# Layer-0 result split straight from its PSUM bank instead of from an SBUF copy, in a fused recommendation tower

## Chip, cores and metric

One core of one Trainium2 chip. The metric is the device time of one execution in microseconds (us), lower is better; a kernel is told by the median of several executions.

## What is computed

For 512 samples, 39 embedding rows of 16 numbers are gathered from tables (`x0`, 39 x 16 for each sample). Three cross layers follow; each multiplies the 39 rows with the rows of the layer before, column by column of the 16, and contracts all pairs with a filter:

```python
e = jnp.stack([tbl_0[ids[:, 0]], ..., tbl_38[ids[:, 38]]], axis=1)   # 512 x 39 x 16
x0, xk = e, e
for W in [f0, f1, f2]:            # 39*39 x 128, 128*39 x 128, 128*39 x 128
    z = jnp.einsum('bfd,bgd->bfgd', x0, xk).reshape(b, f * g, d)
    cur = jnp.einsum('bpd,pm->bmd', z, W)
    outs.append(cur); xk = cur
z = jnp.sum(jnp.concatenate(outs, axis=1), axis=-1)                  # 512 x 384
h = relu(concat([z, dense_ctx]) @ W_top1 + b_top1)
y = relu(h @ W_top2 + b_top2) @ W_top3
```

## The kernel before

**Blocks and tiles.** The 512 samples go in 16 blocks of 32 samples (512 columns, sample by d); a block is four tiles of 128 columns. Layer 0 of block b+1 is made while layer 1 of block b runs. The order on every engine is written out by hand: constants such as `HIGH_AT` name a place (t, n), which is tile t and the n-th group that this engine works on in that tile.

**Layer 0.** SyncE writes the gathered rows to DRAM (`rows_to_dram`) and reads them back in the layout that layer 0 needs (`load_rows`: one DMA into `x0t`, three into `pairs`). `load_rows(b)` waits for `l0_done`, because `pairs` is a single buffer and layer 0 of the block before must have read it. VectorE multiplies `x0t` into `pairs` in seven pieces (`z0`, L435); the first two of block b+2 are made as early as (3, 2) and (3, 3) of block b. Four of the pieces are split into a high and a low fp32r half: ScalarE rounds (`z0h`, L574), VectorE or, for piece 2, GpSimd subtracts (`z0l`, L442 and L383). TensorE sums the seven pieces into the bank `ps0` (`layer0`, called at the places of `L0_AT`, piece 0 at (0, 6), 1 at (0, 8), 4 at (1, 7) and last piece 5 at (2, 3)).

**The layer-0 result** is the left operand of layer 1 and is also split. ScalarE copies the whole bank to SBUF (`load_cur0`, `x1f`, L565), rounds it tile by tile to `x1h` (`high_part`, L581), and VectorE subtracts, `x1l = x1f - x1h` (`low_part`, L449). VectorE also sums `x1f` over d into `s0` (`sum_cur0`, L453). Tiles 0 to 2 are split during block b for block b+1, tile 3 in block b+1 itself: its high part at (0, 0), its low part at (1, 3).

**Layer 1.** In each tile TensorE makes ten groups of four filters, three matmuls each (hi x w1h, hi x w1l, lo x w1h: L769, L770, L773), into a bank of `psd` (two banks) or `psa` (three), by the pattern `adaadadaad`. VectorE takes a "d" group with one tensor_tensor (L474, the first of a tile) or four scalar_tensor_tensor (L486), which frees the bank; ScalarE takes an "a" group with four scaled copies (L618), and GpSimd adds four of those six (L379). GpSimd also makes `x0d` (L364) and starts the gathers of block b+3 (L346). After its first group of a tile, VectorE reduces the four partial results of the tile before (`finish_tile`, L459), for which it waits until ScalarE and GpSimd are through with that tile. One more matmul (`grams`, L747) prepares layer 2.

**After the last block** layer 2 and the small network on top run as before; they reuse `x1f` as the tile `s2`.

Of the kernel before, what the change touches and what calls it, by code (L numbers as in the profile page):

```python
# [25 lines left out]
F32 = mybir.dt.float32  # L26
F32R = mybir.dt.float32r
I32 = mybir.dt.int32
ALU = mybir.AluOpType
# [5 lines left out]
BB = 32  # L35
# [49 lines left out]
assert all(sorted(at.values()) == SPLIT for at in (ZH_AT, ZH_AT_FIRST))  # L85


CUR0_AT, SUM_AT = (2, 3), (2, 3)
HIGH_AT = {(2, 4): 0, (3, 0): 1, (3, 2): 2}
SCALARS_AT = {(2, 5): 0, (3, 1): 1, (3, 3): 2}  # L90
LOW_AT = {(2, 3): 0, (3, 1): 1, (3, 2): 2}
# [36 lines left out]
def build(nc, tables, ids, w0a, w0b, w1, w2, wt1, bt1, wt2, bt2, wt3, dense, mask, ident, out):  # L128
# [4 lines left out]
    with ExitStack() as ctx:  # L133
        def sb(name, shape, dt=F32):
            return ctx.enter_context(nc.sbuf_tensor(name, shape, dt))

        def sem(name):
            return ctx.enter_context(nc.semaphore(name))
# [22 lines left out]
        pairs = sb("pairs", [128, L0T, COLS])  # L161
        z0h = sb("z0h", [128, NS * COLS], F32R)
        z0l = sb("z0l", [128, NS * COLS], F32R)
        x1f = sb("x1f", [128, COLS])
        x1h = sb("x1h", [128, COLS], F32R)
        x1l = sb("x1l", [128, COLS], F32R)

# [15 lines left out]
        h2 = parts[:, 0, 0:H2T, :]  # L183
        wt2_sb = parts[:, 1, 0:H1T * H2T * 128 // B, :].rearrange("p a n -> p (a n)").rearrange("p (k n) -> p k n", k=H1T)
        dense_sb = x0t[0:16, :]
        s2 = x1f
        y_sb = s0[0:1, :]


# [37 lines left out]
        z0l_pool = sem("z0l_pool")  # L227
        l0_done = sem("l0_done")
        tr_done = sem("tr_done")
        x1f_ready = sem("x1f_ready")  # L230
        x1h_ready = sem("x1h_ready")
        x1l_ready = sem("x1l_ready")
        x0c_ready = sem("x0c_ready")
# [191 lines left out]
        def _(dve):  # L425
# [19 lines left out]
            def low_part(b, t):  # L445

                dve.wait_ge(x1h_ready, b * TILES + t + 1)
                c = slice(128 * t, 128 * t + 128)
                dve.tensor_tensor(x1l[:, c], x1f[:, c], x1h[:, c].bitcast(F32), ALU.subtract).then_inc(x1l_ready, 1)  # L449

            def sum_cur0(b, at):
                dve.wait_ge(x1f_ready, b + 1)
                dve.tensor_reduce(s0[:, at], x1f[:, :].rearrange("p (b d) -> p b d", d=D), AX.X, ALU.add)  # L453

            def finish_tile(T, t):

# [6 lines left out]
            def block_of(b, ahead, ahead2, at=None):  # L463
                for t in range(TILES):
                    T = b * TILES + t
                    groups = [g for g in range(NG) if PATTERN[t][g] == "d"]
                    for n, g in enumerate(groups):
# [23 lines left out]
                        if n == 0:  # L491
# [3 lines left out]
                            if t or not starts(b):  # L495
# [1 line left out]
                                dve.wait_ge(pool_adds, bp * NADD + ADD_OFF[tp + 1])  # L497
                                dve.wait_ge(acc_steps, 2 * (bp * ND + D_OFF[tp + 1]))
                                finish_tile(T - 1, tp)
                        if t == 1 and n == 3:  # L500
                            low_part(b, TILES - 1)
                        z0_at = Z0_AT_FIRST if starts(b) else Z0_AT
                        if ahead:
# [24 lines left out]
                dve.tensor_tensor(w1l[:, c], w1raw[:, c], w1h[:, c].bitcast(F32), ALU.subtract).then_inc(w1l_ready, 1)  # L528
            for k in range(L0T):
                z0(0, k)  # L530
            for t in range(3):
                low_part(0, t)
            sum_cur0(0, slice(0, BB))
            block_of(0, True, True, slice(BB, 2 * BB))
            with dve.Fori(1, NBLK - 2) as b:
                block_of(b, True, True, bass.ds((b + 1) * BB, BB))
# [21 lines left out]

        @block.scalar
        def _(act):  # L560
            def load_cur0(b):
                act.wait_ge(l0_done, b + 1)
                if not starts(b):
                    act.wait_ge(x1l_ready, b * TILES)
                act.activation(x1f[:, :], ps0[:, :], ACT.Copy).then_inc(x1f_ready, 1)  # L565
                act.wait_ge(x1f_ready, b + 1)

            def pair_high_part(b, k):

                i = SPLIT.index(k)  # L570
# [5 lines left out]
            def high_part(b, t):  # L576

                c = slice(128 * t, 128 * t + 128)
                if not starts(b):
                    act.wait_ge(y_d, (b - 1) * ND + D_OFF[t + 1])  # L580
                act.activation(x1h[:, c], x1f[:, c], ACT.Copy).then_inc(x1h_ready, 1)  # L581

            def scalars(b, t):
                act.wait_ge(tr_done, b + 1)
# [10 lines left out]
            def block_of(b, ahead):  # L595
                for t in range(TILES):
                    T = b * TILES + t
                    groups = [g for g in range(NG) if PATTERN[t][g] == "a"]
                    for n, g in enumerate(groups):
# [30 lines left out]
                        if t == 0 and n == 2:  # L630
                            scalars(b, 3)
                        if ahead:
                            if (t, n) == CUR0_AT:
                                load_cur0(b + 1)
                            if (t, n) in HIGH_AT:
                                high_part(b + 1, HIGH_AT[t, n])
                            if (t, n) in SCALARS_AT:
                                scalars(b + 1, SCALARS_AT[t, n])
# [11 lines left out]
            for k in range(3):  # L650
                c = slice(k * third, (k + 1) * third)
                act.activation(w1h[:, c], w1raw[:, c], ACT.Copy).then_inc(w1h_ready, 1)
            load_cur0(0)
            for t in range(3):
                high_part(0, t)
            act.wait_ge(w1l_ready, 3)
# [48 lines left out]
        def _(pe):  # L705
            def layer0(b, k):

                if k == 0 and not starts(b):
                    pe.wait_ge(x1f_ready, b)
                pe.wait_ge(z0_ready, b * L0T + k + 1)  # L710
                if k in SPLIT and not starts(b):

                    i = SPLIT.index(k)
                    pe.wait_ge(z0h_ready, (b - 1) * NS + i + 1)
                    if k == ON_POOL:
                        pe.wait_ge(z0l_pool, b)
                    else:
                        pe.wait_ge(z0l_ready, (b - 1) * (NS - 1) + i)
                    c = slice(COLS * i, COLS * i + COLS)
                    w = slice(M * i, M * i + M)  # L720
                    pe.matmul(ps0[:, :], w0h[0:ROWS, w], z0h[0:ROWS, c], start=False, stop=False)  # L721
                    pe.matmul(ps0[:, :], w0h[0:ROWS, w], z0l[0:ROWS, c], start=False, stop=False)
                    op = pe.matmul(ps0[:, :], w0l[0:ROWS, w], z0h[0:ROWS, c], start=False, stop=(k == L0_END))
                    if k == L0_END:
                        op.then_inc(l0_done, 1)
                    return
                rows = F * len(range(SPT * k, min(SPT * k + SPT, SHIFTS)))
                op = pe.matmul(ps0[:, :], w0s[0:rows, k, :], pairs[0:rows, k, :], start=(k == 0), stop=(k == L0_END))  # L728
                if k == L0_END:
                    op.then_inc(l0_done, 1)  # L730
# [70 lines left out]


            pe.wait_ge(mlp_in, 16 * 3)
            pe.wait_ge(x1f_ready, NBLK)
            pe.wait_ge(x0c_ready, NBLK * TILES)
            banks = [ps0, pst, psa[0], psa[1]][:H1T]
            for m, y in enumerate(banks):
# [98 lines left out]
```

## Time and profile before

| | |
|---|---|
| three runs | 773.94, 777.85, 781.08 us; median 777.85 |
| span of the profiled execution | 775.4 us, so 2.45 us under the median |
| VectorE busy | 687.4 us, 89% |
| TensorE matmul busy | 658.1 us, 85% |
| ScalarE busy | 536.4 us, 69% |
| GpSimd busy | 509.0 us, 66% |
| one block in the middle of the run | about 42 us |

The profiled execution has one number, its span; no time of its own beside that is given, so sums are made against the span and carried over to the median. Busy is an average over the whole run. Inside the blocks VectorE is busy for 41.5 of 42 us, and the other engines wait for one another in a fixed pattern that repeats from block to block. A duration shown for an instruction includes time in which it has started and stands still for a resource.

### The profile page before, as it was taken

What the parts mean: (1) busy time and instruction counts of PE and PEld (TensorE: products, weight loads), DVE (VectorE), ACT (ScalarE), POOL (GpSimd) and SP (SyncE); (2) the same over time, 40 slices, a digit from 0 to 9 for tenths busy, and PEclk for the clock granted to TensorE, in tenths of its full rate; (3) what the DMA queues carried; (4) which work ended last, traced back from release to release, by engine and by line L of the source; (5) the groups of instructions that cost most, each with busy time, mean ns of one, the idle gap of its engine ahead of it and who ended that gap; (6) DMA issues with size and microseconds to landing.
All of it is one profiled execution on the core that took longest, in us unless ns stands there. A gap on an engine that the chain in (4) does not pass through costs nothing.

```text
span 775.4 us, 12234 instructions
## 1 busy us (share of the span) xinstructions
PE 658.1 (85%) x2571; PEld 471.9 (61%) x2571; DVE 687.4 (89%) x1110; ACT 536.4 (69%) x1862; POOL 509.0 (66%) x462
## 2 busy tenths in 40 slices
PE   0768888898989888898989898878989898998988
PEld 0246656566766666666766675656666666666563
DVE  1448899999999999999999999979999998999880
ACT  2055768496876767686859686665859696788672
POOL 6755868586767767685868676766868644455340
PEclk9899999999999999999999999998999999999999
DMA  7540404040412214040404031220404041300200
GB/s 190 109 103 6 102 2 100 7 97 8 86 18 54 51 23 82 2 103 1 98 7 96 9 82 23 46 53 7 98 7 96 9 106 31 97 2 1 64 1 0
DMA packets 57049, 40.27 MB, mean 52 GB/s; under 512 B 35455, under 2 KB 39885, under 8 KB 57032
## 3 DMA queue, kind: packets, MB, share of 16 engines
q1 hardware_dynamic: 51206, 38.73, 22.4%
q0 software_dynamic: 5120, 1.29, 1.9%
q10 hardware_dynamic: 706, 0.06, 0.1%
q8 instruction: 6, 0.10, 0.0%
q14 instruction: 11, 0.09, 0.0%
HBM read 38.13 MB, written 1.94 MB: 52 GB/s over the span
## 4 chain that ended last, share of the span: by engine, by line
PE 40%; DMA 18%; issue 17%; DVE 16%; POOL 4%; SPq 2%; ACT 2%; DVEq 1%; ACTq 0%; POOLq 0%
DMA pairs<-x_rows 17%; DVE parts L486 7%; PE psd L769 5%; PE psa L769 4%; PE psa L773 4%; PE psa L770 4%; PE psd L773 4%; PE psd L770 3%; DVE z0l L442 3%; PE ps L728 2%; DVE pairs L435 2%; PE psg L747 2%; PE ps L721 2%; POOL parts L379 1%; ACT prods L618 1%
## 5 line engine op out<-in xcount | busy, mean ns | idle before, releaser
L618 ACT ACTIVATE prods<-psa,x0c 128x128 f32<-128x128 f32 x1024 | 296.8, 393 | 60.5 <-PE psa L773 52.8
L459 DVE TENSOR_REDUCE cur<-parts 128x128 f32<-128x2048 f32 x64 | 245.8, 3840 | 4.1 <-POOL parts L379 3.9
L486 DVE SCALAR_TENSOR_TENSOR parts<-psd,x0c,parts 128x128 f32<-128x128 f32 x704 | 194.3, 342 | 6.4 <-PE psd L773 6.4
L379 POOL TENSOR_TENSOR parts<-parts,prods 128x512 f32<-128x512 f32 x128 | 167.9, 1311 | 40.5 <-ACT prods L618 39.0
L769 PE MATMUL psa<-w1h,x1h 128*128 128x512 f32 x384 | 173.8, 453 | 9.9 <-ACT prods L618 8.8
L346 POOL DMA_INDIRECT emb<-tables,idx x140 | 146.5, 1047 | 32.1 <-issue 19.3
L769 PE MATMUL psd<-w1h,x1h 128*128 128x512 f32 (+1 forms) x256 | 112.6, 440 | 50.0 <-DVE parts L486 48.0
L773 PE MATMUL psa<-w1h,x1l 128*128 128x512 f32 x384 | 152.6, 397 | 0.0
L770 PE MATMUL psa<-w1l,x1h 128*128 128x512 f32 x384 | 152.4, 397 | 0.0
L379 POOL TENSOR_TENSOR parts<-prods 128x512 f32<-128x512 f32 x64 | 84.1, 1313 | 99.2 <-ACT prods L618 89.8
L618 ACT ACTIVATE parts<-psa,x0c 128x128 f32<-128x128 f32 x512 | 143.3, 422 | 2.3 <-ACT x1f L565 2.2
L574 ACT ACTIVATE z0h<-pairs 117x512 fp32r<-117x512 f32 x60 | 38.0, 633 | 117.9 <-DVE pairs L435 116.6
L769 PEld LDWEIGHTS psd<-w1h,x1h 128*128 128x128 f32 x256 | 48.5, 189 | 95.6 <-DVE parts L486 82.5
L435 DVE TENSOR_TENSOR pairs<-x0t,pairs 117x512 f32<-117x512 f32 (+1 forms) x112 | 87.9, 789 | 18.9 <-DMA pairs<-x_rows 18.4
L773 PE MATMUL psd<-w1h,x1l 128*128 128x512 f32 (+1 forms) x256 | 98.4, 384 | 0.0
L770 PE MATMUL psd<-w1l,x1h 128*128 128x512 f32 (+1 forms) x256 | 98.3, 384 | 0.0
L769 PEld LDWEIGHTS psa<-w1h,x1h 128*128 128x128 f32 x384 | 72.6, 189 | 39.9 <-ACT prods L618 16.0
L770 PEld LDWEIGHTS psa<-w1l,x1h 128*128 128x128 f32 x384 | 72.8, 189 | 22.1 <-issue 4.6
L773 PEld LDWEIGHTS psa<-w1h,x1l 128*128 128x128 f32 x384 | 72.5, 189 | 17.9
L449 DVE TENSOR_TENSOR x1l<-x1f,x1h 128x128 fp32r<-128x128 f32 x64 | 56.6, 886 | 4.6 <-ACT x1h L581 4.6
L728 PE MATMUL ps<-pairs,w0s 117*128 117x512 f32 (+1 forms) x104 | 55.8, 627 | 3.8 <-DVE pairs L435 3.7
L474 DVE TENSOR_TENSOR parts<-psd,x0c 128x512 f32<-128x512 f32 x64 | 43.8, 684 | 14.5 <-issue 14.4
(87 smaller groups left out, 753.3 us busy)
## 6 DMA issues: line engine op xcount, KB each, us to landing
pairs<-x_rows SPq DMA_DIRECT2D x30, 546.0 KB
pairs<-x_rows SPq DMA_DIRECT2D x15, 468.0 KB
x0t<-x_rows SPq DMA_DIRECT2D x16, 234.0 KB
emb<-tables,idx POOLq DMA_INDIRECT x140
pairs<-x_rows SPq DMA_DIRECT2D x8, 156.0 KB
x_rows<-emb SPq DMA_DIRECT2D x14, 72.0 KB
wt_sb<-w_top SPq DMA_DIRECT2D x1, 768.0 KB, 12.1
prods<-w SPq DMA_DIRECT2D x1, 704.0 KB, 4.8
```

Source lines behind the costliest of these rows:

```text
L346: pool.indirect_dma_start(emb[0:n, c, :], None, tables, bass.IndirectOffsetOnAxis(idx[0:n, c:c + 1], 0)).then_inc(gathered, 16)
L379: pool.tensor_tensor(parts[:, t % 2, 1, :], first, prods[:, p % P_RING, :], ALU.add).then_inc(pool_adds, 1)
L435: dve.tensor_tensor(pairs[0:rows, k, :], x0t[0:rows, :], pairs[0:rows, k, :], ALU.mult).then_inc(z0_ready, 1)
L449: dve.tensor_tensor(x1l[:, c], x1f[:, c], x1h[:, c].bitcast(F32), ALU.subtract).then_inc(x1l_ready, 1)
L459: dve.tensor_reduce(cur1[:, t % 2, :], parts[:, t % 2, :, :].rearrange("p k (j m) -> p m (k j)", m=M), AX.X, ALU.add).then_inc(c1_ready, 1)
L474: dve.tensor_tensor(parts[:, t % 2, 0, :].rearrange("p (j m) -> p j m", m=M), y[:, :].rearrange("p (j m) -> p j m", m=M), x0c[:, t, GF * g ...
L486: op = dve.scalar_tensor_tensor(acc, y[:, M * j:M * j + M], x0c[:, t, GF * g + j:GF * g + j + 1], acc, ALU.mult, ALU.add)
L618: op = act.activation(dst[:, M * j:M * j + M], y[:, M * j:M * j + M], ACT.Copy, scale=x0c[:, t, GF * g + j:GF * g + j + 1])
L728: op = pe.matmul(ps0[:, :], w0s[0:rows, k, :], pairs[0:rows, k, :], start=(k == 0), stop=(k == L0_END))
L769: pe.matmul(y[:, 0:n], hi, w1h[:, c], start=True, stop=False)
L770: pe.matmul(y[:, 0:n], hi, w1l[:, c], start=False, stop=False)
L773: pe.matmul(y[:, 0:n], lo, w1h[:, c], start=False, stop=True).then_inc(full, 1)
```

## The change

The bank `ps0` is no longer copied to `x1f`; the sum over d, the four high parts and the four low parts read `ps0` itself. ScalarE and VectorE are never to read the bank at the same time, so they take turns by semaphores: the first high part waits for the sum (`s0_summed`), the high part of tile t waits for the low part of tile t-1 (`x1l_ready`), and a low part waits for its high part as before. Layer 0 of the next block overwrites the bank, so its first piece now waits for all four low parts of the block before, where it waited for the copy. The low part of tile 3 is moved from (1, 3) to (0, 0), behind `finish_tile`. In the first block the sum is moved ahead of the low parts. `s2` gets another tile.

```diff
-CUR0_AT, SUM_AT = (2, 3), (2, 3)
+SUM_AT = (2, 3)
 ...
-        s2 = x1f
+        s2 = parts[:, 0, 2, :]
 ...
-                dve.tensor_tensor(x1l[:, c], x1f[:, c], x1h[:, c].bitcast(F32), ALU.subtract).then_inc(x1l_ready, 1)
+                dve.tensor_tensor(x1l[:, c], ps0[:, c], x1h[:, c].bitcast(F32), ALU.subtract).then_inc(x1l_ready, 1)
             def sum_cur0(b, at):
-                dve.wait_ge(x1f_ready, b + 1)
-                dve.tensor_reduce(s0[:, at], x1f[:, :].rearrange("p (b d) -> p b d", d=D), AX.X, ALU.add)
+                dve.wait_ge(l0_done, b + 1)
+                dve.tensor_reduce(s0[:, at], ps0[:, :].rearrange("p (b d) -> p b d", d=D), AX.X,
+                                  ALU.add).then_inc(s0_summed, 1)
 ...
-                        if t == 1 and n == 3:
+                        if t == 0 and n == 0:
                             low_part(b, TILES - 1)
 ...
+            sum_cur0(0, slice(0, BB))
             for t in range(3):
                 low_part(0, t)
-            sum_cur0(0, slice(0, BB))
 ...
-            def load_cur0(b):
-                act.wait_ge(l0_done, b + 1)
-                if not starts(b):
-                    act.wait_ge(x1l_ready, b * TILES)
-                act.activation(x1f[:, :], ps0[:, :], ACT.Copy).then_inc(x1f_ready, 1)
-                act.wait_ge(x1f_ready, b + 1)
 ...
+                if t == 0:
+                    act.wait_ge(s0_summed, b + 1)
+                else:
+                    act.wait_ge(x1l_ready, b * TILES + t)
                 if not starts(b):
                     act.wait_ge(y_d, (b - 1) * ND + D_OFF[t + 1])
-                act.activation(x1h[:, c], x1f[:, c], ACT.Copy).then_inc(x1h_ready, 1)
+                act.activation(x1h[:, c], ps0[:, c], ACT.Copy).then_inc(x1h_ready, 1)
 ...
-                            if (t, n) == CUR0_AT:
-                                load_cur0(b + 1)
 ...
-            load_cur0(0)
 ...
                 if k == 0 and not starts(b):
-                    pe.wait_ge(x1f_ready, b)
+                    pe.wait_ge(x1l_ready, b * TILES)
 ...
-            pe.wait_ge(x1f_ready, NBLK)
+            pe.wait_ge(x1l_ready, NBLK * TILES)
```

## Rows read from the trace of the kernel before

**Rows 1.** The page, costliest groups: line, engine, tiles, count | busy us, mean ns | idle before.

```profile
L449 DVE TENSOR_TENSOR x1l<-x1f,x1h 128x128 fp32r<-128x128 f32 x64 | 56.6, 886 | 4.6 <-ACT x1h L581 4.6
```

**Rows 2.** Single lines of the kernel: count, duration ns min/median/max, first and last start.

```profile
L449 DVE TENSOR_TENSOR x1l<-x1f,x1h x64: 273/972/1511, 40.8 to 700.8; 128x128 fp32r<-128x128 f32 x64
...
L486 DVE SCALAR_TENSOR_TENSOR parts<-psd,x0c,parts x704: 329/341/365, 47.4 to 717.3; 128x128 f32<-128x128 f32 x176
...
L474 DVE TENSOR_TENSOR parts<-psd,x0c x64: 675/680/693, 42.6 to 710.3; 128x512 f32<-128x512 f32 x64
```

**Rows 3.** Chain of waits, 290 to 380 us: start us, us, what.

```profile
288.32 13.49 DMA pairs<-x_rows
...
323.77 0.50 PE psa L769
```

**Rows 4.** Timeline of SyncE's queue: start us, us, instruction; "xN" merges several.

```profile
328.45 0.74 SPq L292 DMA_DIRECT2D x0t<-x_rows  x1
```

**Rows 5.** Timeline of VectorE, one block from `z0` to `z0`.

```profile
301.84 0.69 DVE L435 TENSOR_TENSOR pairs<-x0t,pairs 117x512 f32<-117x512 f32 x1
...
304.43 3.82 DVE L459 TENSOR_REDUCE cur<-parts 128x128 f32<-128x2048 f32 x1
...
312.20 1.18 DVE L435 TENSOR_TENSOR pairs<-x0t,pairs 117x512 f32<-117x512 f32 x1
...
318.27 2.11 DVE L442 TENSOR_TENSOR z0l<-pairs,z0h 117x512 fp32r<-117x512 f32 x1
...
334.25 1.02 DVE L449 TENSOR_TENSOR x1l<-x1f,x1h 128x128 fp32r<-128x128 f32 x1
...
342.13 1.51 DVE L449 TENSOR_TENSOR x1l<-x1f,x1h 128x128 fp32r<-128x128 f32 x1
343.56 0.68 DVE L435 TENSOR_TENSOR pairs<-x0t,pairs 117x512 f32<-117x512 f32 x1
```

**Rows 6.** Timeline of GpSimd beside those VectorE rows.

```profile
301.74 0.92 POOL L346 DMA_INDIRECT emb<-tables,idx  x1 [0.16 <-issue]
...
311.54 1.30 POOL L379 TENSOR_TENSOR parts<-parts,prods 128x512 f32<-128x512 f32 x1
...
317.87 0.74 POOL L364 TENSOR_TENSOR x0d<-x0c,mask_sb 128x320 f32<-128x320 f32 x1
318.55 1.27 POOL L379 TENSOR_TENSOR parts<-parts,prods 128x512 f32<-128x512 f32 x1
...
333.82 1.29 POOL L379 TENSOR_TENSOR parts<-parts,prods 128x512 f32<-128x512 f32 x1
```

**Rows 7.** Timeline of VectorE, last block but two.

```profile
644.01 0.69 DVE L435 TENSOR_TENSOR pairs<-x0t,pairs 117x512 f32<-117x512 f32 x1 [1.98 <-DMA pairs<-x_rows]
```

**Rows 8.** Timeline of ScalarE, end of tile 2 and end of tile 3.

```profile
332.73 0.33 ACT L581 ACTIVATE x1h<-x1f 128x128 fp32r<-128x128 f32 x1
...
339.12 2.30 ACT L618 ACTIVATE parts<-psa,x0c 128x128 f32<-128x128 f32 x8
```

**Rows 9.** Timeline of TensorE in tiles 0 and 1.

```profile
305.57 1.02 PE L728 MATMUL ps<-pairs,w0s 117*128 117x512 f32 x2
...
309.94 0.45 PE L769 MATMUL psd<-w1h,x1h 128*128 128x384 f32 x1 [1.10 <-DVE parts L486]
...
320.44 0.50 PE L721 MATMUL ps<-z0h,w0h 117*128 117x512 f32 x1 [1.74 <-DVE z0l L442]
```

**Rows 10.** Who waited for whom: us in total, times, longest us.

```profile
PE ps L721 <- DVE z0l L442: 23.3, 15, 1.8
PE ps L728 <- DVE pairs L435: 3.7, 1, 3.7
```

**Rows 11.** Busy us by engine and granted clock (third column from the right) behind three such waits.

```profile
56.00:60.00 4.00, 4.00 (x10) 2.42 (x9) 4.00 (x4) 1.66 (x5) 2.25 (x3) 0.57 0.12 14
...
320.00:324.00 4.00, 2.95 (x12) 2.18 (x13) 4.00 (x13) 1.95 (x7) 1.44 (x2) 1.00 0.03 2
362.00:366.00 4.00, 3.87 (x12) 3.02 (x13) 4.00 (x14) 2.25 (x8) 1.45 (x2) 0.71 0.02 2
```

More of the change, by code:

```diff
@@ L163, in build @@
         z0l = sb("z0l", [128, NS * COLS], F32R)
-        x1f = sb("x1f", [128, COLS])
         x1h = sb("x1h", [128, COLS], F32R)
@@ L229, in build @@
         tr_done = sem("tr_done")
-        x1f_ready = sem("x1f_ready")
+        s0_summed = sem("s0_summed")
         x1h_ready = sem("x1h_ready")
```

## Prediction

> **What bounds the kernel now.** I read the page first: VectorE is the busiest engine, and of its groups the one that the change touches looks odd. A low part subtracts 128 columns and takes 886 ns in the mean [rows 1], though the fastest takes 273 and the slowest 1511; operations of VectorE with one operand in PSUM stay within 329 to 365 (L486) and 675 to 693 (L474) through the whole run [rows 2]. The timelines tell why: the low part at 334.25 ends at 335.27, 0.16 us behind GpSimd's addition that ends at 335.11 [rows 5, 6]. A subtraction with both operands in SBUF stands still while GpSimd adds. `z0` and `z0l` are of this kind too: 1.18 and 2.11 us at 312.20 and 318.27, against 0.69 for the `z0` at 301.84, which has only a gather beside it [rows 5, 6]. The Trainium skill (SBUF — State Buffer, Who interferes with whom) says the same of a tensor_tensor with two SBUF inputs against a GpSimd instruction that reads SBUF, and takes it away from one with a single SBUF input.
>
> So the change seems to free 64 x (886 - 280) ns = 39 us of the busiest engine. I don't forecast that, because of the second thing that I read, the chain of waits. It goes through the load: 13.49 us of DMA up to 301.81, and the `z0` at 301.84 starts behind it [rows 3, 5]. The loads form a loop of their own. The load is issued when layer 0 is done, 328.45 [rows 4]; the first `z0` from it starts 15.1 us later, 343.56 [rows 5]. From the `z0` at 301.84 to the next issue are 26.6 us, so a turn is 41.7 us, the block's time. VectorE's own work is as long by coincidence: the low part of 342.13 ends at 343.64 and the `z0` follows at once [rows 5]. In the last block but two, where VectorE is early, it waits for the DMA 1.98 us and gains nothing [rows 7]. Whatever is saved between the end of layer 0 and that `z0` is therefore handed to the DMA; only the 26.6 us count.
>
> **What lies in the hidden part.** The sum and the low parts of tiles 0 to 2. The three low parts took 1.02 + 0.56 (same line, between the rows shown) + 1.51 = 3.1 us [rows 5] and will take 0.3 each (280 ns by the minimum, 340 by L486 [rows 2]; I take 280, since L486's also begins with a wait for its predecessor; the difference is 0.06). Added is a turn between engines: the first high part waits for the sum, 0.33 us [rows 8], and VectorE waits for it at the head of its queue, with the next group's L474 behind it. I take the sum as equally long from either memory, since for 512 columns L474 from PSUM (680) equals a `z0` from SBUF (690) [rows 2, 5]. Net 3.1 - 0.9 - 0.4 = 1.8 us earlier at the `z0`, all of it waiting for the DMA. The page VectorE: DVE Perf Modes (The TRN2 errata) of the Trainium skill lists a PSUM source 62 cycles, 65 ns as an estimate, dearer than one in SBUF; by that the five readers cost 0.3 us a block more, 0.07 of it outside the hidden part; the equal rows speak against it.
>
> ScalarE loses the copy (0.6 us a block, engine two thirds busy: nothing by itself), but is held up twice: its first high part by the sum, by 1.6 us (332.73 [rows 8] to 334.3, where the sum ends and the low part starts [rows 5]), and the third, at (3, 2), until VectorE has done the low part of tile 1, whose group comes after the 3.9 us of `finish_tile`. Behind that high part are three groups of ScalarE. They end at 341.42 now [rows 8]; with high part 3 released at about 340.9, plus 0.33, three groups of 1.15 (half of 2.30) and a copy for `x0c`, they end near 344.7. VectorE needs them for the next `finish_tile`, which comes 2.6 us after `z0` (304.43 after 301.84 [rows 5]), at 346.15: 1.4 us to spare. I cost it at nothing for VectorE; if that cover were gone it would be paid once a block. TensorE gets the three banks later, but its own slack of 1 us before (0, 9) [rows 9] takes it.
>
> **What lies in the 26.6 us.** All times on the block of [rows 5, 9].
> 1. The low part of tile 3 is moved ahead of `z0` piece 2: +0.2 (280 ns, overlapped by 60 with its neighbour). The new wait is free here, ScalarE's high part 3 ends at 304.5, the low part starts at 308.2.
> 2. TensorE's first piece of layer 0 waits for this low part. It stood at 305.57 [rows 9] and now starts at 308.5, since `finish_tile` (304.43 to 308.2 [rows 5]) comes first. TensorE had done piece 0, two groups and piece 1 by 308.8 and then waited 1.10 us for a bank; now it has these 3.1 us of work after 308.5, so group 9 starts at 311.5 instead of 309.94 and its result is there at 312.25. VectorE wants it at 311.65: +0.6.
> 3. The `z0` at 312.20 stood still 0.5 us beside a GpSimd addition. That addition (311.54 to 312.84 [rows 6], 0.2 later with step 1) is tied to the low piece that GpSimd makes, not to TensorE, while the `z0` now comes at 313.0: -0.5.
> 4. `z0l` at 318.27 lost 1.43 us to `x0d` and an addition of GpSimd, 317.87 to 319.82 [rows 5, 6]. These hang on ScalarE's groups of tile 1, so on TensorE, and shift with it by 1.45 us, to 319.3. VectorE arrives at 318.6 (+0.3), when GpSimd is in its gather, which [rows 5, 6] show to be harmless: -1.43. It would have to be 0.7 us later to collide again.
> 5. TensorE's wait for this `z0l` (1.74 us [rows 9]) closes. Layer 0's end then hangs on VectorE's fifth `z0`, ScalarE's high piece and its group, which released L769 at 323.77 [rows 3], all 1.1 us earlier.
>
> Sum: +0.2 + 0.6 - 0.5 - 1.4 = -1.1 us for each of 13 turns, -14 us.
>
> 6. Against it, the clock. TensorE has nothing between 306.0 and 308.5, a pause of 2.5 us that is new. Of the 15 waits of at most 1.8 us for `z0l` [rows 10] two were followed by a granted clock of about 0.7 in the next 4 us, for instance behind 362; the others, as behind 320, were not; the wait of 3.7 us was (0.57) [rows 10, 11]. That is the 1.2 GHz level for part of the time; 0.57 over 4 us is 1.7 us of TensorE's time lost. At this place all of it arrives in step 2, where TensorE is already the late one: with the drop a turn costs -1.1 + 1.7 = +0.6. A pause of 2.5 lies between 1.8 (2 in 15) and 3.7 (always); I take two in three. Mean change of a turn: -1.1 + 0.67 x 1.7 = 0.0.
>
> **Ends.** First block: sum, then high and low parts by turns instead of one after another on two engines, +0.7 us (three added turns of 0.3, less the low parts' overlap). Last blocks without loads are bound by VectorE: two of their low parts were slow (about 1 us together), given back in the turn of engines: 0. The two clock drops of today, at 0.7 each, go with their wait: -1.4. `s2`: nothing.
>
> **Rivals.**
> - A, the clock holds at most new pauses: 13 x -1.1 + 0.7 - 1.4 = -15, 763 us. For: the pause is nearer to 1.8 than to 3.7. Against: two of fifteen shorter ones fell already.
> - B, slower: the pause at layer 0's first piece costs the clock in each block, and `z0l` meets GpSimd's addition again, step 4. Price 1.7 + 1.4 - 1.1 = +2.0 a turn, +26 us, 804; with the clock alone +0.6, 785. It decides from the point where more than nine pauses in ten drop and the later VectorE loses its 0.7 us of margin. The page TensorE: Matmul & The Clock Gate (HAM oscillation) of the Trainium skill tells of a kernel that fell to the low clock at every wait; by that rule it is at least the 785.
> - C, the load doesn't hold VectorE after all, and lands sooner when VectorE is ready sooner: 60 low parts x 0.6 - 14 turns of 0.4 = -30 us, 747. [rows 7] speak against it.
> - D, the change doesn't do what it says: a low part reading `ps0` still stands still for GpSimd. Then the hidden part stays as it is, step 1 costs up to 0.9, and the time is 778 to 790. 704 L486 with no stretched one speak against it [rows 2].
>
> **Numbers.** Forecast: 775.4 + 0 + 0.7 - 1.4 = 774.7 in the profile, 777 us at the median (775.4 is 2.45 below it). Chances: forecast, drops in half to nine tenths of the pauses, 0.42 (770 to 785); A 0.25; B 0.25; C 0.05; D 0.03. Range 761 to 794: it takes in A and the nearer half of B. Faster by over 1% 0.29, within 1% 0.45, slower 0.26; one per cent is about what separates a change from none in this kernel, whose three runs lie 0.9% apart.
>
> **What would show it.** Low parts of 0.27 to 0.34 us in all 64 (else D). VectorE waiting 1 to 2 us for DMA `pairs` in nearly every block, with 15.1 us from L292 to `z0` (else C). L728 of piece 0 waiting for L449 for about 2.5 us in each block. `z0l` at (1, 0) at 0.68 us, or, for B, still 2.1. The clock behind piece 0: counted, it decides between the forecast, A and B. The prediction is wrong if ScalarE's three late groups delay `finish_tile`, or if GpSimd's gathers shift and the load takes longer than 15.1 us.

## Result: 4.5% slower, and the profile after

| | before | after |
|---|---|---|
| median | 777.88 us | 813.75 us (811.39 to 814.72, four runs) |
| ratio | | 1.045, 95% interval 1.0407 to 1.0494 |
| span of the profiled execution | 775.4 us | 811.6 us |
| VectorE busy | 687.4 us | 654.4 us |

The kernel became 36 us slower while its busiest engine lost 33 us of busy time. The forecast was 777 us, with a range to 794.

**The low parts did what they should.** The page of the kernel after; columns as in [rows 1].

```profile
L486 DVE SCALAR_TENSOR_TENSOR parts<-psd,x0c,parts 128x128 f32<-128x128 f32 x704 | 194.4, 341 | 36.8 <-PE psd L767 36.8
L434 DVE TENSOR_TENSOR pairs<-x0t,pairs 117x512 f32<-117x512 f32 (+1 forms) x112 | 100.5, 901 | 36.3 <-DMA pairs<-x_rows 36.3
L722 PE MATMUL ps<-pairs,w0s 117*128 117x512 f32 (+1 forms) x104 | 68.9, 758 | 48.3 <-DVE x1l L448 42.1
```

And a single line of that kernel; columns as in [rows 2].

```profile
L448 DVE TENSOR_TENSOR x1l<-ps,x1h x64: 268/290/318, 38.6 to 724.0; 128x128 fp32r<-128x128 f32 x64
```

All 64 take 268 to 318 ns where they took up to 1511 [rows 2]. But the right-hand column shows three places where VectorE or TensorE now sits idle. Who waited for whom says how often, and adds ScalarE:

```profile
ACT x1h L578 <- DVE s L452: 48.0, 16, 17.5
...
PE ps L722 <- DVE x1l L448: 42.1, 14, 6.7
DVE parts L486 <- PE psd L767: 36.8, 18, 3.8
DVE pairs L434 <- DMA pairs<-x_rows: 36.3, 19, 8.2
```

**One turn of the load loop**, from the issue of a load to the next, in SyncE's queue. It took 46.4 us here. Thirteen turns, from 73.91 to 660.32 us, took 45.1 us each; before, from 75.08 to 627.81, 42.5 us. The difference of 2.6 us times 13 is 34 of the 36 us. So the turn shown is 1.3 us longer than the mean, and the means of all thirteen are given beside its numbers where they differ.

```profile
341.34 0.74 SPq L291 DMA_DIRECT2D x0t<-x_rows  x1
...
387.75 0.74 SPq L291 DMA_DIRECT2D x0t<-x_rows  x1
```

VectorE in this turn; it answers to [rows 5]:

```profile
346.54 0.68 DVE L452 TENSOR_REDUCE s<-ps 128x512 f32 x1
347.65 0.29 DVE L448 TENSOR_TENSOR x1l<-ps,x1h 128x128 fp32r<-128x128 f32 x1 [0.43 <-ACT x1h L578]
...
356.20 2.24 DVE L434 TENSOR_TENSOR pairs<-x0t,pairs 117x512 f32<-117x512 f32 x1 [0.95 <-DMA pairs<-x_rows]
...
360.34 3.69 DVE L459 TENSOR_REDUCE cur<-parts 128x128 f32<-128x2048 f32 x1
363.95 0.27 DVE L448 TENSOR_TENSOR x1l<-ps,x1h 128x128 fp32r<-128x128 f32 x1
...
371.31 0.87 DVE L486 SCALAR_TENSOR_TENSOR parts<-psd,x0c,parts 128x128 f32<-128x128 f32 x3 [3.82 <-PE psd L767]
372.10 0.68 DVE L434 TENSOR_TENSOR pairs<-x0t,pairs 117x512 f32<-117x512 f32 x1
...
377.69 1.24 DVE L441 TENSOR_TENSOR z0l<-pairs,z0h 117x512 fp32r<-117x512 f32 x1
...
379.89 1.43 DVE L434 TENSOR_TENSOR pairs<-x0t,pairs 117x512 f32<-117x512 f32 x1
```

GpSimd beside the `z0` at 356.20, and the same addition in the kernel before:

```profile
355.58 0.98 POOL L345 DMA_INDIRECT emb<-tables,idx  x1 [0.16 <-POOL parts L378]
356.58 1.30 POOL L378 TENSOR_TENSOR parts<-parts,prods 128x512 f32<-128x512 f32 x1
```

```profile
342.18 1.30 POOL L379 TENSOR_TENSOR parts<-parts,prods 128x512 f32<-128x512 f32 x1
```

TensorE at layer 0's first piece; it answers to [rows 9]:

```profile
364.36 2.07 PE L722 MATMUL ps<-pairs,w0s 117*128 117x512 f32 x2 [2.72 <-DVE x1l L448]
366.65 0.63 PE L764 MATMUL psa<-w1l,x1h 128*128 128x512 f32 x1
367.08 0.63 PE L767 MATMUL psa<-w1h,x1l 128*128 128x512 f32 x1
...
369.71 1.12 PE L763 MATMUL psd<-w1h,x1h 128*128 128x384 f32 x1
371.79 0.39 PE L764 MATMUL psa<-w1l,x1h 128*128 128x512 f32 x1
372.02 0.39 PE L767 MATMUL psa<-w1h,x1l 128*128 128x512 f32 x1
```

Read from the load on. From issue to first `z0` are 14.86 us (mean of thirteen 15.2), as before (15.1). VectorE had waited 0.95 us for it, so the time that the low parts gave back did end in the DMA. Then that `z0` takes 2.24 us instead of 0.69: it ends 0.56 us after GpSimd's addition of 356.58. In eleven of the thirteen turns this `z0` took 1.5 us or more, in one 1.13 and in one 0.69; the mean is 1.1 us over the 0.69, against 0.1 before. `finish_tile` comes 4.14 us after this `z0`, not 2.59. Next, TensorE's piece 0 starts after the pause of 2.72 us, and its two matmuls take 2.07 us instead of 1.02 [rows 9]: half speed. The next matmuls start 0.43 us apart (366.65, 367.08), which is half speed too; from 371.79 on it is 0.23 us, full speed again. VectorE gets its group 3.82 us late. The two losses, 1.55 and 3.82, are all but 0.2 of the 5.54 us by which the next `z0` (372.10) is further from the first than before (15.90 against 10.36 us). That `z0` itself is back at 0.68 from 1.18, `z0l` at 1.24 from 2.11, but the `z0` after it stands still for 0.75 us, which it did not (0.68 at 321.34 before).

The clock: 4 us from piece 0 on, columns as in [rows 11], in this block and in one of the two whose pause left the clock up (the other is behind 641.09).

```profile
364.00:368.00 4.00, 3.64 (x7) 2.23 (x8) 3.49 (x12) 0.89 (x2) 2.44 (x3) 0.50 0.00 0
```

```profile
275.00:279.00 4.00, 3.22 (x11) 2.01 (x12) 3.92 (x12) 2.00 (x7) 2.01 (x3) 1.00 0.00 0
```

0.50 is the 1.2 GHz level for all of the 4 us. TensorE waited for the low part in 14 blocks, 13 times for 2.6 to 2.7 us and once for 6.7; the clock fell behind eleven of the 13 and behind the long one. From 98 to 728 us the mean granted clock is 0.96, a shortfall of 25 us; before it was 0.99 and 7 us.

What a fall costs stands in VectorE's wait for group 9: first the block with the clock up, then one with a short fall.

```profile
279.81 0.87 DVE L486 SCALAR_TENSOR_TENSOR parts<-psd,x0c,parts 128x128 f32<-128x128 f32 x3 [0.90 <-PE psd L767]
```

```profile
461.48 0.87 DVE L486 SCALAR_TENSOR_TENSOR parts<-psd,x0c,parts 128x128 f32<-128x128 f32 x3 [2.50 <-PE psd L767]
```

So 0.9 us of this wait come from TensorE's later order alone. A short fall adds 1.6 us, and the longer one of the turn shown 2.9. Over the thirteen turns the wait is 2.4 us in the mean, where the kernel before has none at this place.

Where the new standing still comes from is on ScalarE, tiles 2 and 3 of the block:

```profile
347.34 0.28 ACT L578 ACTIVATE x1h<-ps 128x128 fp32r<-128x128 f32 x1 [2.07 <-DVE s L452]
...
354.13 0.28 ACT L578 ACTIVATE x1h<-ps 128x128 fp32r<-128x128 f32 x1 [1.72 <-DVE x1l L448]
```

ScalarE stops twice, first 2.07 us for the sum. GpSimd adds what ScalarE has made, so the additions of tile 3 come later: the one that matters started 13.7 us after the load's issue before (342.18) and now 15.24 us after it (356.58), which is when the load has landed and `z0` runs. My theory had by then three parts: the first stop puts an addition onto `z0` (1.55 us in this turn, 1.0 more than before in the mean); the pause costs TensorE its clock (about 1.5 us a turn); and what VectorE saves before the load lands is lost in any case. The rivals: the second stop does it; the delay of TensorE's order does it without the clock; or the accumulation bank is in itself dear to read.

### The profile page after: what moved, and what is told of

It is laid out like the page before. It is cut to its first block, busy times and chain, and to the rows that moved or that the text cites. A ratio compares the mean times of both kernels' runs of the same rounds, so it can differ in the third digit from the quotient of the medians.

```text
span 811.6 us, 12250 instructions
## 1 busy us (share of the span) xinstructions
PE 685.1 (84%) x2571; PEld 477.4 (59%) x2571; DVE 654.4 (81%) x1110; ACT 523.5 (64%) x1846; POOL 518.5 (64%) x462
## 4 chain that ended last, share of the span: by engine, by line
PE 40%; issue 20%; DVE 16%; DMA 10%; POOL 5%; ACT 5%; SPq 1%; DVEq 1%; ACTq 1%; POOLq 0%
DMA pairs<-x_rows 9%; DVE parts L486 9%; PE ps L722 7%; PE psa L763 5%; PE psa L767 4%; PE psa L764 4%; PE psd L763 4%; PE psd L767 3%; PE psd L764 3%; POOL parts L378 3%; DVE pairs L434 3%; ACT parts L615 2%; ACT prods L615 2%; DVE z0l L441 2%; PE psg L741 1%
## 5 line engine op out<-in xcount | busy, mean ns | idle before, releaser
L615 ACT ACTIVATE prods<-psa,x0c 128x128 f32<-128x128 f32 x1024 | 301.4, 429 | 43.9 <-PE psa L767 36.8
L486 DVE SCALAR_TENSOR_TENSOR parts<-psd,x0c,parts 128x128 f32<-128x128 f32 x704 | 194.4, 341 | 36.8 <-PE psd L767 36.8
L763 PE MATMUL psa<-w1h,x1h 128*128 128x512 f32 x384 | 182.8, 476 | 28.1 <-ACT prods L615 20.5
L378 POOL TENSOR_TENSOR parts<-parts,prods 128x512 f32<-128x512 f32 x128 | 180.5, 1410 | 21.4 <-ACT prods L615 20.1
L345 POOL DMA_INDIRECT emb<-tables,idx x140 | 142.2, 1016 | 32.3 <-issue 19.3
L764 PE MATMUL psa<-w1l,x1h 128*128 128x512 f32 x384 | 156.0, 406 | 0.0
L767 PE MATMUL psa<-w1h,x1l 128*128 128x512 f32 x384 | 155.9, 406 | 0.0
L763 PE MATMUL psd<-w1h,x1h 128*128 128x512 f32 (+1 forms) x256 | 117.0, 457 | 19.1 <-DVE parts L486 18.5
L434 DVE TENSOR_TENSOR pairs<-x0t,pairs 117x512 f32<-117x512 f32 (+1 forms) x112 | 100.5, 901 | 36.3 <-DMA pairs<-x_rows 36.3
L722 PE MATMUL ps<-pairs,w0s 117*128 117x512 f32 (+1 forms) x104 | 68.9, 758 | 48.3 <-DVE x1l L448 42.1
L578 ACT ACTIVATE x1h<-ps 128x128 fp32r<-128x128 f32 x64 | 20.7, 324 | 73.7 <-DVE s L452 48.0
L474 DVE TENSOR_TENSOR parts<-psd,x0c 128x512 f32<-128x512 f32 x64 | 43.7, 683 | 24.1 <-issue 23.8
```

What stands on the lines that cost most here:

```text
L345: pool.indirect_dma_start(emb[0:n, c, :], None, tables, bass.IndirectOffsetOnAxis(idx[0:n, c:c + 1], 0)).then_inc(gathered, 16)
L378: pool.tensor_tensor(parts[:, t % 2, 1, :], first, prods[:, p % P_RING, :], ALU.add).then_inc(pool_adds, 1)
L434: dve.tensor_tensor(pairs[0:rows, k, :], x0t[0:rows, :], pairs[0:rows, k, :], ALU.mult).then_inc(z0_ready, 1)
L474: dve.tensor_tensor(parts[:, t % 2, 0, :].rearrange("p (j m) -> p j m", m=M), y[:, :].rearrange("p (j m) -> p j m", m=M), x0c[:, t, GF * g ...
L486: op = dve.scalar_tensor_tensor(acc, y[:, M * j:M * j + M], x0c[:, t, GF * g + j:GF * g + j + 1], acc, ALU.mult, ALU.add)
L615: op = act.activation(dst[:, M * j:M * j + M], y[:, M * j:M * j + M], ACT.Copy, scale=x0c[:, t, GF * g + j:GF * g + j + 1])
```

## The experiments

Ratios are to the kernel before, run on the same chip, with 95% intervals. First the change in steps.

**The low part of tile 3 moved, alone** (m1_move, on the kernel before):

```diff
-                        if t == 1 and n == 3:
+                        if t == 0 and n == 0:
                             low_part(b, TILES - 1)
```

> The kernel before, with the low part of tile 3 moved from (1, 3) to (0, 0) and nothing else. Theory 1 (the loss comes from TensorE's wait for this low part at layer 0's first piece, and from the clock that this pause costs): the move alone has no wait behind it and puts at most one stretched low part of 0.3 to 1 us ahead of the z0l that the load hangs on: 0 to +10 us. Theory 2 (the order of VectorE's operations alone brings its subtractions beside GpSimd's additions): more than half of the 36 us is here already.

Measured: 782.91 us, 1.0061 (1.0027 to 1.0094): 3 us, where step 1's +0.2 a turn makes 2.6. So the order of VectorE's operations alone is not the loss.

**With TensorE's wait** (m2_move_wait, the move and):

```diff
                 if k == 0 and not starts(b):
-                    pe.wait_ge(x1f_ready, b)
+                    pe.wait_ge(x1l_ready, b * TILES)
```

> The kernel before with the moved low part and with TensorE's new wait: layer 0's first piece of the next block waits for all four low parts. Everything is still read from the SBUF copy, and nobody takes turns. Theory 1: most of the loss is here, +20 to +36 us over before, with a pause of 2.5 us or more ahead of the first piece in each block and the clock at its lower level behind nearly each. Theory 3 (the turns between ScalarE and VectorE at the bank make the loss): within 1% of the run with the move alone.

Measured: 797.25 us, 1.0224 (1.014 to 1.0307). Who waited for whom in it:

```profile
PE ps L728 <- DVE x1l L449: 42.7, 14, 7.1
DVE parts L486 <- PE psd L773: 31.8, 16, 3.6
```

These are the waits of the kernel after (42.1 and 36.8), with the copy to `x1f` and everything else still as before. The clock's shortfall is 20 us, with falls behind ten of 14 pauses. So this one wait makes the pause, the clock falls and VectorE's wait for group 9. It costs 17 us, half of the loss and less than the 20 to 36 us expected. The first `z0` of a load still takes 0.69 us here in nearly every turn.

**With the low parts from the bank** (m3_low_psum, m2_move_wait and):

```diff
-                dve.tensor_tensor(x1l[:, c], x1f[:, c], x1h[:, c].bitcast(F32), ALU.subtract)...
+                dve.tensor_tensor(x1l[:, c], ps0[:, c], x1h[:, c].bitcast(F32), ALU.subtract)...
```

> As the run before it, but the low parts read the PSUM bank; high parts and sum still read the copy in SBUF, so no turns. What is left between this and the changed kernel is the turns and the missing copy. Theory 1: the freed time of the low parts is waited away at the load, so this is within 1% of the run with move and wait. Theory 3: it is near the time of before, and the changed kernel is 20 us or more above it. If VectorE's own work set the pace after all, it is 20 us or more under the run with move and wait.

Measured: 802.06 us, 1.0299 (1.0191 to 1.0406), with low parts of 268 to 309 ns. The 0.8% above m2_move_wait is within the two intervals; whether it is anything stays open. The clock's shortfall is 24 us here. What is clear is that short low parts gave no time.

**Short low parts without the pause** (h1_hybrid, on the kernel before): tiles 0 to 2 from the bank, tile 3 from `x1f` at its old place.

```diff
+                src = x1f if t == TILES - 1 else ps0
-                dve.tensor_tensor(x1l[:, c], x1f[:, c], ...
+                dve.tensor_tensor(x1l[:, c], src[:, c], ...
 ...
                     pe.wait_ge(x1f_ready, b)
+                    pe.wait_ge(x1l_ready, b * TILES - 1)
```

> The kernel before, where only the low parts of tiles 0 to 2 read the PSUM bank; tile 3 reads the SBUF copy at its old place, TensorE waits for the low parts of tiles 0 to 2 only (long done by then). No turns, no new pause. Load theory (what lies between the end of layer 0 and the first z0 is handed to the DMA): within 1% of before, VectorE waiting for the DMA 1 to 2 us a block. VectorE theory: 45 low parts of 0.6 us less, -20 to -27 us.

Measured: 781.37 us, 1.0005 (0.9965 to 1.0044). The line, and whom VectorE waits for:

```profile
L450 DVE TENSOR_TENSOR x1l<-ps,x1h x48: 279/287/296, 41.6 to 687.0; 128x128 fp32r<-128x128 f32 x48
```

```profile
DVE pairs L435 <- DMA pairs<-x_rows: 42.8, 16, 7.1
```

The three low parts of a block are short and nothing is gained; VectorE's wait for the load goes from 18.4 to 42.8 us. The load holds the block.

**Take the load away as the bound** (s1_split_load, on the kernel before): the rows of pieces 0 and 1 in DMAs of their own, first, so that the early `z0` need not wait for all.

```diff
+EARLY, REST = 2, ((0, 2, 4), (0, 4, 7), (1, 2, 7), (2, 2, 6))
 ...
                 for k in range(SPT):
-                    n = len(range(k, SHIFTS, SPT))
-                    ... sp.dma_start(pairs[F * k:F * k + F, 0:n, :], src).then_inc(loaded, 16)
+                    load_piece(k, 0, EARLY, loaded)
+                for k, first, end in REST:
+                    load_piece(k, first, end, loaded_rest)
 ...
+                if k == (FIRST_PIECES[-1][0] if starts(b) else EARLY):
+                    dve.wait_ge(loaded_rest, 16 * LOAD_DMAS * (b + 1))
```

> The kernel before, where the load's two early pieces (all that the z0 at (3, 2) and (3, 3) read) come in DMAs of their own, ahead of the others and with a semaphore of their own. Load theory: VectorE's waits for DMA go from 18 us to under 10, but its own work is as long as the loop was, so within 1% of before. If the load loop alone set the pace: 10 us or more less.

Measured: 772.29 us, 0.991 (0.9881 to 0.994). VectorE's wait for the load falls to 9.9 us, and the mean of thirteen turns from 42.5 to 42.05 us (the commonest turn is 41.66).

**Both** (s2_split_hybrid, the two edits before this together):

> Split load together with the low parts of tiles 0 to 2 read from the bank. Load theory: only both together give the freed time of VectorE away as time, 13 to 15 blocks x 1.2 to 1.8 us, -16 to -27 us against before. Rival (something else, such as ScalarE or TensorE, is as close as the load): within 1% of before as each of the two alone.

Measured: 767.66 us, 0.9851 (0.9806 to 0.9895). Less than expected. VectorE in tile 3, then GpSimd:

```profile
336.39 0.29 DVE L460 TENSOR_TENSOR x1l<-ps,x1h 128x128 fp32r<-128x128 f32 x1
336.58 2.42 DVE L445 TENSOR_TENSOR pairs<-x0t,pairs 117x512 f32<-117x512 f32 x1
```

```profile
336.15 0.98 POOL L354 DMA_INDIRECT emb<-tables,idx  x1 [0.16 <-POOL parts L387]
337.14 1.30 POOL L387 TENSOR_TENSOR parts<-parts,prods 128x512 f32<-128x512 f32 x1
```

`z0` comes at once behind the low part, 1.9 us sooner, but now stands still for the very addition for which the low part had. It does so in eleven of thirteen turns, so most of what came sooner is lost again. Curing the one operation hands its stall to the next with two operands in SBUF.

**The clock by itself** (f1_fill, on the kernel after): eight matmuls that compute nothing, into a bank that is free and overwritten later, in the pause.

```diff
+                        if ahead and not starts(b) and (t, g) == (0, 6):
+                            pe.wait_ge(act_prods, b * NA + a - A_RING + 1)
+                            for _ in range(8):
+                                pe.matmul(psa[a % A_RING][:, :], hi, w1h[:, 0:512], start=True, stop=True)
```

> The changed kernel with eight matmuls of 512 columns more in each block, in TensorE's pause ahead of layer 0's first piece; they write into the bank that the next group overwrites, so no result depends on them. The pause shrinks from 2.7 to about 0.9 us, the wait itself stays as long. Clock theory: the clock stays up, g9 of tile 0 comes 1.7 us or more earlier, 13 x 1.7 = 22 us less than the changed kernel, about 792. Wait theory (the wait alone makes TensorE late, the clock is a side effect hidden elsewhere): within 1% of the changed kernel.

Measured: 794.65 us, 1.0204 (1.0156 to 1.0252). The pause that is left is 0.97 us, and from 98 to 534 us the granted clock is 1.00, without a fall. It falls once later, behind the one wait of 4.9 us; the shortfall from 98 to 728 us is 2 us, not 25. The clock in one block, then VectorE's waits:

```profile
354.00:358.00 4.00, 3.42 (x14) 2.15 (x13) 4.00 (x6) 2.60 (x10) 2.94 (x3) 1.00 0.28 30
```

```profile
DVE parts L486 <- PE psd L767: 18.9, 17, 2.8
```

Against 1.045 the fillers are worth 2.5%, 19 us (by the two intervals 14 to 24): that is what the low clock cost. VectorE's wait for group 9 is 0.9 us in nearly every block, as in the two blocks of the kernel after whose clock stayed up, for TensorE's order is as late as there.

**Layer 0's first pieces later in TensorE's order** (g1_later, on the kernel after):

```diff
-L0_AT = {(0, 6): 0, (0, 8): 1, ...
+L0_AT = {(0, 8): 0, (0, 9): 1, ...
```

> The changed kernel with layer 0's first two pieces moved two groups and one group back, from (0, 6) and (0, 8) to (0, 8) and (0, 9), so that TensorE has two groups of work, 1.4 us, while it would wait. If wait and clock are the loss: the pause falls to about 1.3 us, the clock holds, group 9 waits for one piece less, 795 or less. If the turns between ScalarE and VectorE are the loss: within 1% of the changed kernel.

Measured: 792.71 us, 1.0183 (1.0133 to 1.0233).

```profile
PE ps L722 <- DVE x1l L448: 22.2, 14, 4.5
...
DVE parts L486 <- PE psd L767: 2.3, 2, 1.5
```

Two groups now stand ahead of piece 0. VectorE's wait for TensorE is gone, the pause is about 1.4 us, and the clock's shortfall falls to 10 us: the clock did not quite hold, it fell behind four of twelve such pauses. The `z0` at (3, 2) still takes 1.2 to 2.3 us in all but two of the thirteen turns.

**ScalarE's second stop moved** (t1_turn, on the kernel after): high and low part 2 one place later.

```diff
-HIGH_AT = {(2, 4): 0, (3, 0): 1, (3, 2): 2}
+HIGH_AT = {(2, 4): 0, (3, 0): 1, (3, 3): 2}
-LOW_AT = {(2, 3): 0, (3, 1): 1, (3, 2): 2}
+LOW_AT = {(2, 3): 0, (3, 1): 1, (3, 3): 2}
```

> The changed kernel with the split of tile 2 one group later on both engines (high and low part at (3, 3) instead of (3, 2)), so that ScalarE no longer waits 1.7 us for the low part of tile 1 ahead of three groups. If this second stop of ScalarE makes the loss between the run with low parts from the bank and the changed kernel: 10 us or more less than the changed kernel. Theory of the first stop (ScalarE's 2.07 us at the sum start all of GpSimd's additions of tile 3 late, and the last one falls beside the z0 at (3, 2)): within 1% of the changed kernel, since that addition is bound by the one before it and not by ScalarE's late group; z0 at (3, 2) still 1.5 to 2.4 us.

Measured: 819.7 us, 1.0454 (1.0387 to 1.0521), the ratio of the kernel after. VectorE, then GpSimd, then ScalarE; `z0` still stands beside the addition.

```profile
317.06 1.83 DVE L434 TENSOR_TENSOR pairs<-x0t,pairs 117x512 f32<-117x512 f32 x1 [1.59 <-DMA pairs<-x_rows]
```

```profile
317.02 1.30 POOL L378 TENSOR_TENSOR parts<-parts,prods 128x512 f32<-128x512 f32 x1
```

```profile
314.55 0.28 ACT L578 ACTIVATE x1h<-ps 128x128 fp32r<-128x128 f32 x1 [0.66 <-DVE x1l L448]
319.97 0.28 ACT L578 ACTIVATE x1h<-ps 128x128 fp32r<-128x128 f32 x1 [1.90 <-DVE x1l L448]
```

The stop ahead of the addition is cut from 1.72 to 0.66 us and nothing is gained. But the edit is not clean: the high part of tile 3 now stops ScalarE for 1.90 us behind the `z0`. What settles the second stop is the next run.

**ScalarE's first stop removed** (t2_sum, on the kernel after): high part 0 and low part 0 ahead of the sum; the same readers of the bank in another order.

```diff
-                        if ahead and (t, n) == SUM_AT:
-                            sum_cur0(b + 1, at)
                         if ahead and (t, n) in LOW_AT:
                             low_part(b + 1, LOW_AT[t, n])
+                        if ahead and (t, n) == SUM_AT:
+                            sum_cur0(b + 1, at)
 ...
                 if t == 0:
+                    act.wait_ge(l0_done, b + 1)
+                elif t == 1:
                     act.wait_ge(s0_summed, b + 1)
```

> The changed kernel with the order of the turns changed: high part 0, low part 0, then the sum, then high part 1 (first block too), so that ScalarE doesn't wait for the sum in tile 2. Theory of the first stop: GpSimd's additions of tile 3 come 1.5 us earlier against the load, z0 at (3, 2) takes 0.7 us again, 13 x 1.3 us = 17 us less than the changed kernel, ratio to before 1.02 to 1.03. Rival (second stop): within 1% of the changed kernel.

Measured: 795.57 us, 1.0159 (1.0114 to 1.0204). VectorE, then GpSimd, then ScalarE:

```profile
313.70 0.69 DVE L434 TENSOR_TENSOR pairs<-x0t,pairs 117x512 f32<-117x512 f32 x1 [1.77 <-DMA pairs<-x_rows]
```

```profile
312.20 1.29 POOL L378 TENSOR_TENSOR parts<-parts,prods 128x512 f32<-128x512 f32 x1
```

```profile
310.81 0.28 ACT L581 ACTIVATE x1h<-ps 128x128 fp32r<-128x128 f32 x1 [2.80 <-DVE x1l L448]
```

The addition ends at 313.49, 0.2 us before `z0`, which takes 0.69 us again; the mean over thirteen turns is 0.1 us above that. The second stop has grown to 2.80 us and does no harm, so the first stop was the cause. The clock still falls in 11 blocks. 2.9%, 22 us (by the two intervals 18 to 28), hung on where the sum stands among the readers. The two profiled executions lie only 15 us apart, and 13 of them are the first `z0`; that is the surer number for this cause, and what else the ratio holds stays open.

**Both causes removed** (g5_late_sum: t2_sum with the order of g1_later):

> Both mends: layer 0's first two pieces later, as in the run before with them at (0, 8) and (0, 9), and the sum behind low part 0. If the two losses are separate they add up: ratio 1.018 less 0.02, so 0.995 to 1.005, about the time of before. If the standing still beside GpSimd only moves to another subtraction: 1.01 or more.

Measured: 779.02 us, 0.998 (0.9954 to 1.0006).

```profile
DVE pairs L434 <- DMA pairs<-x_rows: 37.6, 18, 5.9
...
DVE parts L486 <- PE psd L770: 2.3, 2, 1.5
```

No copy, all low parts short, VectorE's wait for group 9 gone, and the time of the kernel before. Together the two edits take off 4.7% (2.9 and 2.7 alone, which overlap). So the addition on the `z0` and TensorE's wait, with the clock that it costs, account for the whole loss. Ahead of the `z0` the load is why nothing is gained: VectorE waits 37.6 us for it. Behind it, from `z0` to the next issue, a turn takes 27.35 us in the mean against 27.25 before, so nothing is gained there either, although `z0l` stands still less; no run isolates why.

**A faster one** (k1_split_hybrid_z0, on s2_split_hybrid): both early `z0` in one place.

```diff
-EARLY_Z0_AT = {(3, 2): 0, (3, 3): 1}
+EARLY_Z0_AT = {(3, 3): (0, 1)}
```

> The run with split load and low parts of tiles 0 to 2 from the bank, with both early z0 behind group 9 at (3, 3). There the z0 at (3, 2) stood still 1.7 us for the addition that the low part before it had stood for. 0.8 us later less of this addition is left: if the standing still is tied to the addition and not to the operation, z0 takes 1.5 to 1.7 us instead of 2.4, and 13 x 0.8 = 10 us go, ratio 0.97 to 0.975. If VectorE's freed time is lost in another way, 0.98 to 0.99 as before.

Measured: 759.32 us, 0.9703 (0.9661 to 0.9745). VectorE, then GpSimd:

```profile
335.67 2.24 DVE L445 TENSOR_TENSOR pairs<-x0t,pairs 117x512 f32<-117x512 f32 x2
```

```profile
335.45 1.30 POOL L387 TENSOR_TENSOR parts<-parts,prods 128x512 f32<-128x512 f32 x1
```

One addition is now paid for by two multiplications that take 2.24 us together, where one alone took 2.42; the first of them takes about 1.6 us, as expected. The commonest turn is 40.74 us, the mean 41.4. No run has this order of the `z0` without the short low parts, so what each gives is not separated. The kernel is 21 us faster than the kernel before on the same chip (780.61), and by the two ratios 7% faster than the kernel after (0.9703 / 1.045).

## Why the prediction was wrong, step by step

**Right.** "What lies in the hidden part": the load loop was the bound. The low parts take 18 us in all where they took 57 [rows 1], and VectorE's wait for the load grew from 18 to 36 us. h1_hybrid (1.0005) shows it with nothing else changed, with 43 us of that wait. Rival C is out. The low parts take 0.29 us (rival D out). The Trainium skill (VectorE: DVE Perf Modes, The TRN2 errata) would make them an estimated 65 ns dearer from PSUM; their median in h1_hybrid is 14 ns above the fastest from SBUF (287 to 273), so the 65 were rightly left out. Step 1 is small (m1_move, +0.6%). Step 2's pause is there in 14 blocks, 2.72 us where 2.5 was written. Step 3's `z0` is back at 0.68 (372.10). Step 5: TensorE's wait for `z0l` fell from 23.3 us [rows 10] to 1.7.

**Wrong: "I cost it at nothing" for ScalarE's two stops.** I asked only whether ScalarE's groups would be ready for `finish_tile`, and they nearly were (5.1 us of waits for them in the whole run). I did not follow them to GpSimd. Its addition moved from before the load's landing onto the `z0` behind it, up to 1.6 us in a turn and 1.0 more than before in the mean, inside the 26.6 us that count. In step 3 I had followed one of GpSimd's additions, but not this one. t2_sum gives the 1.0 us a turn back in its rows, and 22 us by its ratio. It also shows that the first stop is the cause, for the second is longer there.

**Mis-sized: step 6, "I take two in three".** The clock fell behind 12 of 13 pauses, and each time for 3.5 us or about 7, not 1.7 us lost every time. The term was 0.67 x 1.7 = 1.1 us a turn; f1_fill measures 19 us, 1.5 a turn. Of my two bounds, always for 3.7 us and 2 in 15 up to 1.8, a pause of 2.7 lay at the first, and the price was that of a whole window at 0.50, where I had taken 0.57 and none longer.

**Mis-sized: steps 3 and 4, "-0.5" and "-1.43".** `z0l` was to fall to 0.68; it took 1.24 here, and the `z0` behind it lost 0.75. Over thirteen turns the `z0l` stand still 0.7 us less than before, and the later `z0` of a turn in sum as long as before. So -0.7 came where -1.9 was forecast. The clock is not the reason, for in f1_fill, where it holds, `z0l` and these `z0` stand still as long. What remains is that the stalls move to the next exposed operation, as in s2_split_hybrid; no run isolates it here.

**Mis-sized: step 6, "0.67 x 1.7".** The clock fell behind 12 of 14 pauses, which is in the forecast's "half to nine tenths"; a short fall costs 1.6 us and a long one 2.9, where 1.7 was written. The term was 1.1 us a turn; f1_fill measures 19 us, 1.5 a turn, and so do the waits for group 9.

**Mis-sized: step 2, "+0.6".** TensorE's work from 305.57 to 308.84 is 3.3 us, not 3.1, and with it the step's own rows give +0.9. With the clock up VectorE waits 0.90 us (279.81).

**The sum.** Mean us of a turn from the first `z0` to the next issue, as the timelines have them:

| | forecast | measured |
|---|---|---|
| first `z0` beside the addition | 0 | +1.0 |
| wait for group 9, from the order (step 2) | +0.6 | +0.9 |
| wait for group 9, from the clock (step 6) | +1.1 | +1.5 |
| `z0l` and later `z0` (steps 3 and 4) | -1.9 | -0.7 |
| the rest | +0.2 | 0.0 |
| all | 0.0 | +2.7 |

The part ahead of the `z0` is 0.1 us shorter than before, which leaves the 2.6. In the rest, VectorE's low part of tile 3 is 0.7 us shorter and its waits ahead of L474, for which the profile names no cause, are 0.6 us longer. Rival B (804) was nearest, partly by luck: it had the clock and one more collision with GpSimd's addition, at 1.4 us, but at `z0l`, which in fact stood still less than before. The time was outside of the range because only the nearer half of B was in it, and because no rival had the `z0` in it.

## What to carry to other kernels

An operation that stands still for another engine is not cured by making it immune: the conflict passes to the next one that is not, so list what will run beside each of the partner's instructions afterwards. A wait put on an engine off the critical path moves everything that its followers feed; follow it to the last one (ScalarE, then GpSimd, then VectorE), not to the first that looks safe. And before removing work from the busiest engine, find the loop that sets the period: here short low parts alone gave nothing (h1_hybrid), and 3% came with the split load, the short low parts and the moved `z0` together (k1_split_hybrid_z0).

## What was not expected of the hardware

- Being the first to start does not always help. In the kernel after, `z0` starts at 356.20, 0.38 us before GpSimd's addition at 356.58, and ends 0.56 us after its end; in s2_split_hybrid 0.56 us before (336.58 and 337.14), with the same result. By the Trainium skill (SBUF — State Buffer, Who interferes with whom) the one that starts first has the port for its whole instruction and the other blocks; here it was the first, VectorE's, that stood, and the addition kept its 1.30 us. But the kernel before has the opposite too, VectorE, then GpSimd:

```profile
303.23 0.69 DVE L435 TENSOR_TENSOR pairs<-x0t,pairs 117x512 f32<-117x512 f32 x1
```

```profile
303.55 1.51 POOL L379 TENSOR_TENSOR parts<-prods 128x512 f32<-128x512 f32 x1 [0.90 <-ACT prods L618]
```

  Here the first one kept its time and the addition stood. What differs in the traces is what GpSimd did just before. Over all runs, a `z0` or `z0l` that started up to 0.6 us ahead of an addition took 1.9 to 2.4 us in 40 of 41 cases where the addition followed a gather at once, and 0.67 to 0.69 us in all 60 cases where GpSimd had been idle ahead of it; there the addition took up to 1.79 us. Why is not shown; the start that the profile records may not be the moment at which the port is taken. A `z0` beside a gather with no addition close behind takes 0.69 us [rows 5, 6].
- Pauses of TensorE of 2.6 to 2.9 us were followed by the 1.2 GHz level 11 times in 13 in the kernel after, and 49 times in 64 over it, m2_move_wait, m3_low_psum, t1_turn and t2_sum. Those of at most 1.8 us [rows 10] were 2 times in 15, those of 1.4 us in g1_later 4 times in 12, and those of 0.6 to 1.0 us in f1_fill none of 13 times. The low level lasted some 3.5 us, in some blocks about 7.
- Reading the accumulation bank cost VectorE nothing to speak of: the sum takes 0.68 us from it (346.54), as from SBUF before (at 333.66), and the low part 0.29.
